# A gated graph network on one core: the state transposes of 33 units taken from TensorE to VectorE block transposes and DMA

## The reference

```python
# layer L0: y = (adj x + x) W + b, each row divided by its length
# layer L1: five steps of a gated unit, state h = x at the start
m  = einsum('nm,bmd->bnd', adj, h)                # used twice, as m_in and m_out
u3 = h @ u3_w.T + u3_b
z  = sigmoid(concat(m, m) @ w3_w.T + w3_b + u3)
r  = sigmoid(concat(m, m) @ w4_w.T + w4_b + u3)
hv = tanh(concat(m, m) @ w5_w.T + w5_b + ((r * h) @ u5_w.T + u5_b))
h  = (1 - z) * h + z * hv
# layer L2: normalised adjacency (adj + I), then W;  layer L3: softmax over adj > 0, two weights
```

## Time and profile before

| what | value |
|---|---|
| median of 3 runs | 758.38 us (758.14 to 758.45) |
| profiled execution, its own time | 758.88 us |
| its span | 756.8 us |
| TensorE busy | 748.6 us, 99% |
| VectorE busy | 634.8 us, 84% |
| ScalarE busy | 506.2 us, 67% |
| GpSimd busy | 161.2 us, 21% |
| moved by DMA | 17.21 MB, mean 23 GB/s |

### The profile page before, as it was taken

The page is one execution under the profiler, slowest core; times in us unless marked ns, Lnnn a source line. Parts: engine busy times, 40 slices in busy tenths (PEclk is TensorE's granted clock), DMA queues, the critical chain, the costliest instruction groups (busy, mean ns, idle before and its releaser), DMA issues.

```text
span 756.8 us, 11720 instructions
## 1 busy us (share of the span) xinstructions
PE 748.6 (99%) x3780; PEld 627.8 (83%) x3780; DVE 634.8 (84%) x1463; ACT 506.2 (67%) x1057; POOL 161.2 (21%) x307
## 2 busy tenths in 40 slices
PE   9999999999999999999999999999999999999996
PEld 8888788888888888888888888888888888888886
DVE  5898888899887999877777887777999999897775
ACT  4899777866667666666666666666587858874433
POOL 1878221100000000000000000000122258764333
PEclk9999999999999999999999999999999999999999
DMA  6500000000012101000000000000000000001112
GB/s 215 220 1 2 1 1 0 1 1 0 1 35 85 15 1 56 1 0 1 1 1 0 1 1 1 0 1 1 0 1 1 1 1 1 2 29 42 57 43 84
DMA packets 11612, 17.21 MB, mean 23 GB/s; under 512 B 4512, under 2 KB 6048, under 8 KB 10912
## 3 DMA queue, kind: packets, MB, share of 16 engines
q1 hardware_dynamic: 11552, 16.47, 6.5%
HBM read 9.12 MB, written 5.25 MB: 19 GB/s over the span
## 4 chain that ended last, share of the span: by engine, by line
PE 92%; ACT 5%; DVE 1%; issue 1%; DMA 1%; SPq 0%; POOL 0%; POOLq 0%; ACTq 0%; DVEq 0%
PE agg_ps L1087 14%; PE agg_ps L1089 14%; PE agg_ps L1088 14%; PE gate_ps L1010 7%; PE gate_ps L1012 7%; PE gate_ps L1011 7%; PE cand_ps L1010 5%; PE cand_ps L1012 5%; PE cand_ps L1011 5%; PE turn_ps L1126 5%; PE gate_ps L1017 3%; PE cand_ps L1017 3%; ACT feat L531 1%; PE turn_ps L1130 1%; ACT res L445 1%
## 5 line engine op out<-in xcount | busy, mean ns | idle before, releaser
L1087 PE MATMUL agg_ps<-adj_hi,nat_hi 128*128 128x512 f32 x384 | 152.1, 396 | 0.0
L1089 PE MATMUL agg_ps<-adj_hi,nat_lo 128*128 128x512 f32 x384 | 150.2, 391 | 0.0
L1088 PE MATMUL agg_ps<-adj_lo,nat_hi 128*128 128x512 f32 x384 | 149.6, 390 | 0.0
L646 POOL TENSOR_SCALAR shift<-mean_var 128x4 f32<-128x4 f32 x62 | 23.6, 380 | 423.3 <-DVE mean_var L872 421.3
L822 DVE TENSOR_TENSOR agg_lo<-agg_ps,agg_hi 128x512 fp32r<-128x512 f32 x80 | 55.0, 688 | 59.9 <-ACT agg_hi L474 59.9
L516 ACT ACTIVATE reset_hi<-gate_r 128x512 fp32r<-128x512 f32 x80 | 50.6, 633 | 78.9 <-DVE gate_r L839 78.9
L497 ACT ACTIVATE gate_r<-gate_ps,bias 128x512 f32<-128x512 f32 x80 | 55.2, 690 | 48.1 <-PE gate_ps L1012 48.1
L1089 PEld LDWEIGHTS agg_ps<-adj_hi,nat_lo 128*128 128x128 f32 x384 | 72.0, 188 | 16.3
L1088 PEld LDWEIGHTS agg_ps<-adj_lo,nat_hi 128*128 128x128 f32 x384 | 72.2, 188 | 15.7
L1087 PEld LDWEIGHTS agg_ps<-adj_hi,nat_hi 128*128 128x128 f32 x384 | 72.1, 188 | 15.2
L474 ACT ACTIVATE agg_hi<-agg_ps 128x512 fp32r<-128x512 f32 x80 | 48.2, 602 | 40.9 <-PE agg_ps L1089 40.6
(11 more groups left out here) (205 smaller groups left out, 1760.0 us busy)
## 6 DMA issues: line engine op xcount, KB each, us to landing
res<-in_x SPq DMA_DIRECT2D x16, 256.0 KB, 6.3
out<-res SPq DMA_DIRECT2D x16, 256.0 KB, 2.0
rows<-in_adj SPq DMA_DIRECT2D x4, 256.0 KB, 4.8
adj_hi<-eye_hi SPq DMA_DIRECT2D x1, 1024.0 KB, 9.9
adj_lo<-eye_lo SPq DMA_DIRECT2D x1, 1024.0 KB, 11.7
later<-in_adj SPq DMA_DIRECT2D x1, 1024.0 KB, 6.2
mix_rows<-mix SPq DMA_DIRECT2D x1, 1024.0 KB, 7.8
later<-mix_rows SPq DMA_DIRECT2D x1, 1024.0 KB, 4.7
```

What stands on the lines that cost most here:

```text
L1087: pe.matmul(ps, nat_hi[:, b, k, :], m_hi[:, k, :], start=(k == 0), stop=False)
L1088: pe.matmul(ps, nat_hi[:, b, k, :], m_lo[:, k, :], start=False, stop=False)
L1089: last = pe.matmul(ps, nat_lo[:, b, k, :], m_hi[:, k, :], start=False, stop=(k == T - 1))
```

## The change

The states of units 45 to 77 (`BY_DMA`) are no longer transposed on TensorE. In slot `u+3` VectorE transposes the 32 x 32 blocks of the state into `cand[:, u % 2, :]`, writing with a step of 4 elements; SyncE stores that to `swap_dram` with four DMAs of 64 KB (32 partitions each, 2 KB pieces), and one unit later fetches it back, block columns turned, into `nat_lo` with four DMAs of 64 KB in 512-byte pieces. ScalarE copies `nat_lo` to `nat_hi` in slot `u+5`, VectorE makes the low part in place in slot `u+6`. ScalarE's tanh, which writes the same `cand` buffer two units later, now waits for the store (`swap_out`). TensorE reads the weights of these units with a step of 4 elements. SyncE's new loop stands behind L401. VectorE's step instructions of all 80 units of L1 have another order.

```diff
--- before.py
+++ after.py
@@ -39,6 +39,9 @@
 L0, L2, L3 = 0, STEPS + 1, STEPS + 2
 UNITS = B * (STEPS + 3)
 LAST = B * STEPS
+BY_DMA = range(45, 78)
+BLOCK = 32
+BLOCKS = P // BLOCK
 AFTER = B * (STEPS + 1)
 STATE_LAG = 4
@@ -135,7 +138,7 @@
     found = []
-    if is_inner(s - STATE_LAG):
+    if is_inner(s - STATE_LAG) and s - STATE_LAG not in BY_DMA:
         found.append(("state", s - STATE_LAG))
     if s == ADJ_AT:
         found.append(("adj", 0))
@@ -160,6 +163,21 @@
 TURN_NO = {x: i for i, x in enumerate(TURNS)}
+SWAP_LAG = 5
+
+TURNED = [u for u in range(B, LAST) if u not in BY_DMA]
+
+
+def swaps(u):
+
+    return 16 * BLOCKS * sum(v <= u and v % 2 == u % 2 for v in BY_DMA)
+
+
+def dense(s):
+
+    return s - SWAP_LAG - 1 in BY_DMA
+
+
 def read_by_act(turn):
     return turn[0] == "back" and stage(turn[1]) == L0
@@ -309,6 +327,8 @@
         z_made, cand_made = sem("z_made"), sem("cand_made")
         diff_made, move_made, state_made = sem("diff_made"), sem("move_made"), sem("state_made")
         turned = sem("turned")
+        swapped, swap_hi_made, swap_lo_made = sem("swapped"), sem("swap_hi_made"), sem("swap_lo_made")
+        swap_out, swap_in = ([sem(f"{n}{i}") for i in range(2)] for n in ("swap_out", "swap_in"))
         turn_read, turn_read_act, rows_read = sem("turn_read"), sem("turn_read_act"), sem("rows_read")
         state_hi_made = sem("state_hi_made")
         squared, length_made, shift_made = sem("squared"), sem("length_made"), sem("shift_made")
@@ -400,6 +420,26 @@
             sp.wait_ge(l2_lo_made, T)
             sp.dma_start(later[:, :, :], mix_dram.rearrange("(p t) m -> p t m", t=T)).then_inc(mix_loaded, 16)
+            def swap_back(u):
+
+                sp.wait_ge(swap_out[u % 2], swaps(u))
+                back = [v for v in BY_DMA if v < u and v % 2 == u % 2]
+                if back:
+                    sp.wait_ge(swap_in[u % 2], swaps(back[-1]))
+                rows_of = swap_dram[u % B].rearrange("(a i) (q c) -> q i a c", a=BLOCKS, q=BLOCKS)
+                for q in range(BLOCKS):
+                    sp.dma_start(flat(nat_lo[q * BLOCK:(q + 1) * BLOCK, u % B, :, :]).rearrange("i (a c) -> i a c", a=BLOCKS)
+                                 .bitcast(F32), rows_of[q]).then_inc(swap_in[u % 2], 16)
+
+            for u in BY_DMA:
+                sp.wait_ge(swapped, nth(BY_DMA, u))
+                for a in range(BLOCKS):
+                    part = slice(a * BLOCK, (a + 1) * BLOCK)
+                    sp.dma_start(swap_dram[u % B, part, :], cand[part, u % 2, :]).then_inc(swap_out[u % 2], 16)
+                if u - 1 in BY_DMA:
+                    swap_back(u - 1)
+                if u + 1 not in BY_DMA:
+                    swap_back(u)
             sp.wait_ge(mix_loaded, 16)
             sp.wait_ge(shares_made, 2)
             sp.dma_start(mix_dram[0:2].rearrange("a (t p) -> p a t", p=P), shares[:, :, :],
@@ -485,7 +525,9 @@
                 u = s - 2
                 if is_step(u):
                     act.wait_ge(cand_done, u - B + 1)
-                    if u >= B + 2:
+                    if u - 2 in BY_DMA:
+                        act.wait_ge(swap_out[u % 2], swaps(u - 2))
+                    elif u >= B + 2:
                         act.wait_ge(state_made, u - B - 1)
                     act.activation(cand[:, u % 2, :], cand_ps[u % 2][:, :], ACT.Tanh,
                                    bias=bias[:, B_H:B_H + 1]).then_inc(cand_made, 1)
@@ -515,12 +557,17 @@
                         act.wait_ge(cand_done, u - B)
                     act.activation(reset_hi[:, :], gate_r[:, u % 2, :], ACT.Copy).then_inc(reset_hi_made, 1)
                 u = s - STATE_LAG
-                if is_inner(u):
+                if is_inner(u) and u not in BY_DMA:
                     k = TURN_NO["state", u]
                     act.wait_ge(turned, k + 1)
                     act.wait_ge(agg_done, u + 1)
                     act.activation(nat_hi[:, u % B, :, :], turn_ps[k % 2][:, :].rearrange("p (t d) -> p t d", t=T),
                                    ACT.Copy).then_inc(state_hi_made, 1)
+                u = s - SWAP_LAG
+                if u in BY_DMA:
+                    act.wait_ge(swap_in[u % 2], swaps(u))
+                    act.activation(flat(nat_hi[:, u % B, :, :]), flat(nat_lo[:, u % B, :, :]).bitcast(F32),
+                                   ACT.Copy).then_inc(swap_hi_made, 1)
                 for n in norms_at(s, "norm"):
                     if stage(n) != L0 and n < UNITS - 1:
                         norm(n, T // 2, T)
@@ -821,35 +868,53 @@
                     dve.wait_ge(agg_hi_made, s + 1)
                     dve.tensor_tensor(agg_lo[:, s % 2, :], agg_ps[s % 2][:, :], agg_hi[:, s % 2, :].bitcast(F32),
                                       ALU.subtract).then_inc(agg_lo_made, 1)
+                u = s - 3
+                if u in BY_DMA:
+                    dve.wait_ge(state_made, u - B + 1)
+                    dve.transpose(cand[:, u % 2, :].rearrange("p (q d k) -> p k q d", q=BLOCKS, k=T),
+                                  feat[:, u % B, :].rearrange("p (k q i) -> p k q i", q=BLOCKS, k=T)).then_inc(swapped, 1)
                 u = s - 2
                 if is_step(u):
                     dve.wait_ge(cand_made, u - B + 1)
                     dve.tensor_tensor(cand[:, u % 2, :], cand[:, u % 2, :], feat[:, u % B, :],
                                       ALU.subtract).then_inc(diff_made, 1)
+                u = s - 1
+                if is_step(u):
+                    dve.wait_ge(r_made, u - B + 1)
+                    dve.tensor_tensor(gate_r[:, u % 2, :], gate_r[:, u % 2, :], feat[:, u % B, :],
+                                      ALU.mult).then_inc(reset_made, 1)
+                u = s - 2
+                if is_step(u):
                     dve.wait_ge(diff_made, u - B + 1)
                     dve.wait_ge(z_made, u - B + 1)
                     dve.tensor_tensor(cand[:, u % 2, :], cand[:, u % 2, :], gate_z[:, u % 2, :],
                                       ALU.mult).then_inc(move_made, 1)
+                u = s - SWAP_LAG - 1
+                if u in BY_DMA:
+                    dve.wait_ge(swap_hi_made, nth(BY_DMA, u))
+                    dve.tensor_tensor(flat(nat_lo[:, u % B, :, :]), flat(nat_lo[:, u % B, :, :]).bitcast(F32),
+                                      flat(nat_hi[:, u % B, :, :]).bitcast(F32), ALU.subtract).then_inc(swap_lo_made, 1)
+                if is_step(s) and not dense(s):
+                    dve.wait_ge(feat_hi_made, s - B + 1)
+                    dve.tensor_tensor(feat_lo[:, :], feat[:, s % B, :], feat_hi[:, :].bitcast(F32),
+                                      ALU.subtract).then_inc(feat_lo_made, 1)
+                u = s - 2
+                if is_step(u):
                     dve.wait_ge(move_made, u - B + 1)
                     dve.tensor_tensor(feat[:, u % B, :], feat[:, u % B, :], cand[:, u % 2, :],
                                       ALU.add).then_inc(state_made, 1)
                 u = s - 1
                 if is_step(u):
-                    dve.wait_ge(r_made, u - B + 1)
-                    dve.tensor_tensor(gate_r[:, u % 2, :], gate_r[:, u % 2, :], feat[:, u % B, :],
-                                      ALU.mult).then_inc(reset_made, 1)
-                if is_step(s):
+                    dve.wait_ge(reset_hi_made, u - B + 1)
+                    dve.tensor_tensor(reset_lo[:, :], gate_r[:, u % 2, :], reset_hi[:, :].bitcast(F32),
+                                      ALU.subtract).then_inc(reset_lo_made, 1)
+                if is_step(s) and dense(s):
                     dve.wait_ge(feat_hi_made, s - B + 1)
                     dve.tensor_tensor(feat_lo[:, :], feat[:, s % B, :], feat_hi[:, :].bitcast(F32),
                                       ALU.subtract).then_inc(feat_lo_made, 1)
-                u = s - 1
-                if is_step(u):
-                    dve.wait_ge(reset_hi_made, u - B + 1)
-                    dve.tensor_tensor(reset_lo[:, :], gate_r[:, u % 2, :], reset_hi[:, :].bitcast(F32),
-                                      ALU.subtract).then_inc(reset_lo_made, 1)
                 u = s - STATE_LAG
-                if is_inner(u):
-                    dve.wait_ge(state_hi_made, u - B + 1)
+                if is_inner(u) and u not in BY_DMA:
+                    dve.wait_ge(state_hi_made, nth(TURNED, u))
                     dve.tensor_tensor(nat_lo[:, u % B, :, :],
                                       turn_ps[TURN_NO["state", u] % 2][:, :].rearrange("p (t d) -> p t d", t=T),
                                       nat_hi[:, u % B, :, :].bitcast(F32), ALU.subtract).then_inc(turn_read, 1)
@@ -1068,7 +1133,10 @@
                     if s < B:
                         pe.wait_ge(x_lo_made, s + 1)
                     elif 2 * B <= s < AFTER:
-                        pe.wait_ge(turn_read, reads(TURN_NO["state", s - B]))
+                        if s - B in BY_DMA:
```

(15 more changed lines are left out.)

## The result

| | before | changed |
|---|---|---|
| median | 758.31 us (758.14 to 758.45, 4 runs) | 765.98 us (764.55 to 767.22, 4 runs) |
| profiled execution, its span | 758.88, 756.8 | 764.55, 762.5 |

The ratio is 1.01, 95% interval 1.0085 to 1.0114.

What follows compares the result with a forecast made beforehand. TensorE, 99% busy, was taken as the bound, with its r gate wait hiding the transposes' price. 758.88 - 3.0 - 1.0 + 4.8 + 1.8 = 761.5, less 0.5 for the median: 761.0 us; own range 759.9 to 762.4, full range 756.4 to 768.

Steps and rivals of the forecast that it cites:

- the forecast's own mechanism: Slots 49 to 81: gains of 3.0 and 1.0 us, outweighed by one first-store wait and low clock, 4.8 and 1.8 us.
- the rival of longer steady slots: Slots with DMA states: slow block transpose, strided loads or late fetch lengthen every slot, giving 767, 772 or 794 us; chance 0.19.
- the signs named for a wrong forecast: PE's wait in slot 49 under 3 us, or dense slots shorter than 6.45 or longer than 6.6 us.
- Part 1: TensorE, slots 49 to 81: transposes go, but the r gate wait remains; 33 x 0.09 = 3.0 us less.
- Part 2: VectorE's new order brings `reset_lo` earlier in slots 19, 23, 25, 27 and 93: 1.0 us less, bounds 0 and 2.0.
- Part 3, the block transpose: VectorE in a steady slot: 0.69 us, bounds 0.69 and 1.38, covered up to 1.2 us, nothing on the path.
- Part 3, the strided loads: TensorE's step-of-four weight loads: 206 ns, hidden under 227 ns matmuls; upper bound 255 ns, showing 11 us.
- third rival: Steady slots longer through block transpose, strided loads (255 ns, 11 us more, 772) or late fetch; chance 0.19.
- Part 3, DMAs: Steady slots: store lands 2.0 us after issue, fetch between 2.0 and 4.7; both hidden, the fetch with 0.7 us to spare.
- Part 4: Slot 49: tanh waits for the first store behind L401, 4.8 us more once; TensorE's clock falls, 1.8 us more.
- The faster rival: Slot 49's store passes L401's packets, least wait 3.1 us, and the new order gives 2.0: 756.5 us; chance 0.13.
- the short wait: Slot 49's store lands at 300.7 to 302.4 without loss of clock: about 758.3 us, the same; chance 0.25.

Runs made afterwards that it cites:

- the late product: On the changed kernel with the 1 MB load behind the stores, TensorE takes the product waiting for the r gate one slot later: 748.48 us, ratio 0.9869.
- the version without it: Changed kernel with the 1 MB load of `later` moved behind SyncE's new loop, so nothing precedes the first store: 757.90 us, ratio 0.9995.
- both halves strided: Load behind the stores, r gate's product later, dense slots' `reset_lo` and `feat_lo` before the new state, both weight halves read with step four: 746.29 us, ratio 0.9833.

## Why the prediction was right or wrong

The direction and the place of the loss were right, its size was not. 761.0 was forecast and 765.98 measured: 7.7 us more than before, where the sum gave 2.7. That lies inside the stated range of 756.4 to 768, but outside the 759.9 to 762.4 that the forecast's own mechanism was given; the wide range had its upper part for the rival of longer steady slots, and one of that rival's three causes came. One of the signs named for a wrong forecast came too, dense slots longer than 6.6 us (6.62 from slot 61 on). By its steps:

- **Part 1 (3.0 us less) held, mechanism and size.** Slots 50 to 59 take 6.51 us as slot 88 did, with PEld waiting 0.52 us for the r gate, and with contiguous weights slots 50 to 81 are 2.8 us shorter than before. That this wait was the reason is shown by the late product: it took 9.4 us off (757.90 to 748.48) with the states by DMA and 0.5 us without.
- **Part 2 (1.0 us less): 1.0 us by the order alone, and in slots 18 to 28 of the changed kernel.** Right.
- **Part 3, the block transpose: 1.08 us against the 0.69 I took** (bounds 0.69 and 1.38). Its cover of 1.2 us held, so it cost nothing, as said.
- **Part 3, the strided loads, is the step that failed.** "I take hidden" was wrong, and so was the upper bound of 255 ns: they take 310 ns. It was drawn from loads for transposes (L968, with the same step), by adding their penalty of 67 ns to 188; the penalty here is 122 ns. The price was 3.5 us (contiguous weights), not the 11 us of the third rival. Wrong as well, the other way, was the rule that what a load takes beyond the 227 ns of its matmul shows in full: at 310 ns that would be 83 ns a matmul, 33 us in all, but the matmuls are 8 ns farther apart, since the loads overlap one another. In the rival's 11 us these two errors work against each other. The Trainium skill, SBUF — State Buffer, "Door 1: The DMA port swizzle", has a penalty for each access that crosses into a new 16-byte line. The runs agree, on three engines: loads take 310 against 188 ns, and with `nat_hi` put in contiguous order VectorE's subtraction 1.10 against 0.69 us and ScalarE's copy 1.12 against 0.62.
- **Part 3, DMAs:** a store landed 1.7 and a fetch 2.0 us after its issue; both hidden, as said.
- **Part 4 (4.8 us and 1.8 us of clock): slot 49 cost 7.0 us** in the profile, 8.1 in the median of the version without it. The wait was there, released by that store, and the clock fell. The wait was 5.7 us, above the upper bound of 5.5: the tanh was held for 6.6 us, not 5.5, since the store landed 5.9 us after its first issue instead of the 5.1 counted. What made it later is not shown; the load took 5.4 us instead of 4.7 to land, and the store of the next unit was issued straight behind. The clock cost 1.4 us in this profile and 2.4 in two others, around the 1.8 taken. That price was drawn from eight matmuls at the start, where the windows show a granted clock of 1.00, so those rows did not show that the clock was the reason. The pace is that of the rows at 0.50, where matmuls are 0.43 us apart; how many would run so, seven here and twelve in the two others, was a guess at eight.

Summed: 761.0 + 3.5 (the loads) + 1.5 (slot 49, 8.1 instead of 4.8 + 1.8) = 766.0, against 765.98. The terms are known to some tenths, so the exact agreement is chance. The faster rival fell, since the wait could not be short; the short wait fell too, with 5.7 us of waiting and a lost clock. The expectation of a median 8 us lower for a kernel that hands over one unit less was met.

## What to carry to other kernels

A busy share of 99% doesn't say what work is worth: before pricing work that is to leave the busiest engine, find a place in the trace where it is absent (here one slot in forty) and see what the engine does there instead. Here it waited for ScalarE. Moving one load took the change from 1% slower to no difference; filling that wait made it 1.3% faster, and a further change of order and contiguous `nat_hi` 1.9%. When a stream of DMAs is put behind an older one in program order, check the first of them against its reader's deadline: one late buffer cost 8.1 us, against gains of 4 us.

## What was not expected of the hardware

- A weight load of 128 x 128 in `fp32r` with a step of four elements takes 310 ns instead of 188, and twelve in a row keep matmuls of 512 columns 0.235 us apart instead of 0.227.
- Behind a transpose the first such load shows more: with both halves strided the next matmul starts 0.43 us after it (523.21 to 523.64), with contiguous `nat_hi` 0.31 (522.04 to 522.35). Slots take 6.83 us against 6.66.
- VectorE pays for the same step: a subtraction with it takes 1.10 us, 0.69 without; ScalarE's copy 1.12 instead of 0.62. The block transpose that writes with the step takes 1.08 us; no run has one without it, so how much of that is the step is not shown.
- The clock did not fall at the same point of the same wait: with TensorE idle from 297.5 the granted clock was 0.50 from 299.5 on, and with contiguous weights, idle from 297.9, it was still 1.00 at 302.0.
